# A 2-layer macaron model on one core: the routing and tiles 41 to 52 of the second expert pass take other places in the five engine queues

## The reference, cut to what matters

```python
x = L0_attn_hidden_states                               # 16 x 256 x 128, float32
x = x + 0.5 * _L0_ffn_ref(_layernorm(x), ...)           # 8 experts, top 1: the first passage
x = x + _L0_attn_ref(_layernorm(x), ...)                # conv, q/k/v, cumulative pooling, feed-forward
x = x + 0.5 * _L0_ffn_ref(_layernorm(x), ...)           # the same 8 experts: the second passage
x = x + 0.5 * _L1_ffn_ref(_layernorm(x), ...)           # 16 experts with a capacity
x = x + _L1_attn_ref(_layernorm(x), ...)                # a recurrence along the sequence
x = x + 0.5 * _L1_ffn_ref(_layernorm(x), ...)

def _L0_ffn_ref(x, wr, br, w1, b1, w2, b2):
    expert_id = jnp.argmax(jnp.einsum('bsh,he->bse', x, wr) + br, axis=-1)
    h = gelu(jnp.einsum('bsh,ehf->ebsf', x, w1) + b1)   # 128 -> 512
    y = jnp.einsum('ebsf,efh->ebsh', h, w2) + b2        # 512 -> 128
    return jnp.einsum('ebsh,bse->bsh', y, one_hot(expert_id, 8))
```

## Time and profile before

| | before |
|---|---|
| median of 3 runs | 665.62 us (664.96 to 666.88) |
| the profiled execution | 665.63 us, of which the span is 663.6 |
| PE busy | 612.0 us, 92% of the span |
| DVE busy | 448.8 us, 68% |
| POOL busy | 367.2 us, 55% |
| ACT busy | 323.4 us, 49% |
| mean granted clock of TensorE | 0.957 |

### The profile page before, as it was taken

The page is one execution under the profiler, slowest core; times in us unless marked ns, Lnnn a source line. Parts: engine busy times, 40 slices in busy tenths (PEclk is TensorE's granted clock), DMA queues, the critical chain, the costliest instruction groups (busy, mean ns, idle before and its releaser), DMA issues.

```text
span 663.6 us, 13121 instructions
## 1 busy us (share of the span) xinstructions
PE 612.0 (92%) x3647; PEld 472.9 (71%) x3647; DVE 448.8 (68%) x1882; ACT 323.4 (49%) x1037; POOL 367.2 (55%) x377
## 2 busy tenths in 40 slices
...
GB/s 268 316 153 263 190 210 203 106 50 253 127 60 71 115 42 70 238 201 190 205 254 136 97 147 110 79 144 136 179 11 143 146 57 60 169 115 156 94 100 14
DMA packets 87030, 94.17 MB, mean 142 GB/s; under 512 B 12156, under 2 KB 65439, under 8 KB 86704
## 3 DMA queue, kind: packets, MB, share of 16 engines
...
## 4 chain that ended last, share of the span: by engine, by line
PE 57%; DVE 12%; POOL 12%; DMA 8%; issue 8%; ACT 3%; SPq 1%; ACTq 0%; DVEq 0%; POOLq 0%
PE ps L907 8%; PE ps L900 8%; PE ps L835 8%; PE ps L827 8%; POOL xs L1620 8%; PE ps L932 4%; PE ps L784 3%; PE ps L882 3%; PE ps L745 3%; PE ps L849 3%; POOL y L1624 2%; PE ps L875 2%; DMA y<-yt,xi 2%; PE ps L890 1%; PE ps L914 1%
## 5 line engine op out<-in xcount | busy, mean ns | idle before, releaser
L1620 POOL DMA_INDIRECT xs<-X,IDX x128 | 125.6, 981 | 97.9 <-issue 64.8
L1513 ACT ACTIVATE ht<-ps,CL 128x128 f32<-128x128 f32 x336 | 93.1, 379 | 97.1 <-PE ps L827 97.0
L1624 POOL DMA_INDIRECT y<-yt,xi x84 | 83.1, 989 | 50.1 <-DVE yt L1253 34.7
L827 PE MATMUL ps<-xt,w1s 128*128 128x128 f32 x672 | 86.7, 278 | 1.9 <-DVE xt L1247 1.2
L835 PE MATMUL ps<-W,ht 128*128 (+1 forms) x672 | 86.2, 279 | 2.1 <-ACT ht L1513 1.9
L835 PEld LDWEIGHTS ps<-W,ht 128*128 128x128 f32 x672 | 81.4, 195 | 4.3 <-issue 4.2
L827 PEld LDWEIGHTS ps<-xt,w1s 128*128 128x128 f32 x672 | 80.2, 192 | 4.3 <-DVE xt L1247 2.2
L1611 POOL TENSOR_TENSOR sma<-sma,MH 128x4 f32<-128x4 f32 (+1 forms) x24 | 30.6, 1279 | 69.9 <-DVE sma L962 63.8
L932 PE MATMUL ps<-MT,KC 128*128 128x512 f32 x114 | 55.8, 646 | 0.4
L1570 ACT ACTIVATE hb<-ps 128x320 f32<-128x320 f32 x64 | 26.7, 428 | 49.1 <-PE ps L900 48.8
L1253 DVE SCALAR_TENSOR_TENSOR yt<-ps,xb 128x128 f32<-128x128 f32 x84 | 23.9, 287 | 35.0 <-PE ps L835 33.9
(11 more groups left out here) (214 smaller groups left out, 1299.0 us busy)
## 6 DMA issues: line engine op xcount, KB each, us to landing
...
```

Source lines behind the costliest of these rows:

```text
L827: r = e.matmul(ps[TILE_BANKS[i % n]][:, c * P:(c + 1) * P], W1[i % NW1][:, c * P:(c + 1) * P], XTT[i % NX][:, :], start=True, stop=True)
L1513: r = e.activation(HT[i % NHT][:, c, :], ps[TILE_BANKS[i % len(TILE_BANKS)]][:, c * P:(c + 1) * P], ACT.Gelu, bias=CL[:, bass.ds(r0 * 4 + ...
L1620: return e.indirect_dma_start(dst, bass.IndirectOffsetOnAxis(ap=IDX[:, n:n + 1], axis=0), X[:, n, 0:w], None, bounds_check=hi, oob_is_err= ...
L1624: return e.indirect_dma_start(dst, bass.IndirectOffsetOnAxis(ap=ix, axis=0), src, None, bounds_check=hi_home, oob_is_err=False, engine_sem ...
```

## The change

Only `TABLE` changes. On each of the five lists the steps are the same as before, in another order: on SP places 100 to 144 of 275, on PE 214 to 322 of 766, on DVE 280 to 430 of 865, on ACT 109 to 159 of 382, on POOL 92 to 138 of 304. In words:

- PE: `pscore.8` to `pscore.10` go ahead by some ten places, in between `ak.5`, `aconv.7` and `aturn3.4`; `rrank.2` stands ahead of `ak.6`, `av.6`, `adown.3`, `aturn4.4`, `aturn4.5`, `aturn3.6` and `aup.16` to `aup.18`, not behind them; `tturn.41` to `tup.46` begin earlier among the last attention steps, `adown.7`, `pturn.12`, `pscore.13` to `pscore.15` come later; `rrank.4` stands behind `tup.47` and `tturn.48`, and `tturn.51` ahead of `tup.48`.
- DVE: `pstat.10`, `peps.0`, `plog.3`, `oh.3`, `ra.2`, `rb.2` and `rsel.2` go ahead of attention steps of chunks 4 to 7; the tile steps of 41 to 52 are spread otherwise.
- ACT: a few neighbours change places (`tgelu.41` ahead of `aaff3.7`, `pcopy.11` behind `agelu.30`).
- POOL: `apow3.6` stands behind seven sends, not ahead of all; `ppow` steps move; `home.45` ahead of `send.52`, `home.46` to `home.51` in one run.
- SP: `tload.52` to `tload.58` and `tw.46` to `tw.58` are interleaved otherwise; `tload.53` ahead of `tw.48`.

The diff, cut where both sides are only wrapped otherwise:

```diff
--- before.py
+++ after.py
@@ "sp" @@
-tw.36 tw.37 tw.38 tw.39 tw.40 yload.3 yload.4 yload.5 yload.6 yload.7 fill.0 fill.1 fill.2 fill.3 fill.4 fill.5 fill.6 fill.7 fill.8 fill.9 fill.10
-tw.41 tload.41 tload.42 tload.43 tload.44 tload.45 tload.46 tload.47 tload.48 tw.42 tw.43 tw.44 tw.45 tload.49 tload.50 tload.51 wload.0 wload.1 tw.46
-tw.47 tload.52 tw.48 tw.49 tload.53 tload.54 tw.50 tw.51 tload.55 tw.52 tw.53 tload.56 tw.54 tw.55 tload.57 tload.58 tw.56 tload.59 tw.57 tw.58
+tw.36 tw.37 tw.38 tw.39 tw.40 yload.3 yload.4 yload.5 yload.6 yload.7 fill.0 fill.1 fill.2 fill.3 fill.4 fill.5 fill.6 fill.7 fill.8 fill.9 tw.41
+fill.10 tw.42 tload.41 tload.42 tload.43 tload.44 tload.45 tload.46 tload.47 tload.48 tw.43 tw.44 tload.49 tload.50 tw.45 tw.46 tw.47 tload.51 wload.0
+tload.52 tload.53 wload.1 tw.48 tw.49 tw.50 tw.51 tload.54 tload.55 tload.56 tload.57 tload.58 tw.52 tw.53 tw.54 tw.55 tload.59 tload.60 tw.56 tw.57
+tw.58 tload.61 tload.62 tw.59 tw.60 tw.61 tw.62 tw.63 tload.63 tload.64 tw.64 tload.65 tw.65 tw.66 tload.66 tload.67 tload.68 tw.67 tw.68 tload.69
...
@@ "pe" @@
-aturn2.5 aup.11 aq.4 ak.4 av.4 aturn4.3 adown.2 aq.5 aturn1.7 ak.5 pturn.7 aconv.7 aturn2.6 aturn3.4 av.5 aup.12 aup.13 aturn3.5 aq.6 aup.14 aup.15
-pscore.8 pscore.9 pscore.10 ak.6 av.6 adown.3 aturn4.4 aturn4.5 aturn3.6 aup.16 aup.17 aup.18 rrank.2 aup.19 aturn2.7 adown.4 aq.7 aup.20 aup.21
-aup.22 aup.23 aturn4.6 ak.7 pturn.8 pturn.9 pscore.11 pscore.12 av.7 aup.24 aup.25 aup.26 aturn3.7 aup.27 rrank.3 adown.5 adown.6 aturn4.7 pturn.10
-pturn.11 aup.28 aup.29 aup.30 tturn.41 aup.31 tturn.42 tup.41 tturn.43 adown.7 pscore.13 pscore.14 tturn.44 pturn.12 tup.42 tturn.45 tdown.41 tup.43
-tturn.46 pscore.15 tup.44 tdown.42 tturn.47 tdown.43 tdown.44 rrank.4 tup.45 tup.46 tup.47 tturn.48 tdown.45 tdown.46 tdown.47 tturn.49 tturn.50
-tup.48 tturn.51 tup.49 tup.50 tdown.48 tdown.49 tturn.52 tdown.50 tup.51 tturn.53 tup.52 tup.53 tturn.54 tdown.51 tdown.52 tdown.53 tturn.55 tup.54
-tturn.56 tup.55 tup.56 tturn.57 tdown.54 tdown.55 tturn.58 tdown.56 tturn.59 tup.57 tup.58 tturn.60 tturn.61 tup.59 tdown.57 tdown.58 tdown.59
+aturn2.5 aup.11 aq.4 ak.4 av.4 aturn4.3 adown.2 aq.5 pturn.7 aturn1.7 ak.5 pscore.8 aconv.7 pscore.9 aturn3.4 pscore.10 av.5 aup.12 aturn2.6 aup.13
+aturn3.5 aq.6 aup.14 aup.15 rrank.2 ak.6 av.6 adown.3 aturn4.4 aturn4.5 aturn3.6 aup.16 aup.17 aup.18 aup.19 aturn2.7 aup.20 adown.4 aup.21 aq.7
+aup.22 aup.23 aturn4.6 pturn.8 pturn.9 ak.7 aup.24 pscore.11 pscore.12 av.7 aup.25 aturn3.7 aup.26 aup.27 rrank.3 adown.5 tturn.41 tturn.42 tup.41
+tturn.43 adown.6 aturn4.7 pturn.10 pturn.11 aup.28 aup.29 aup.30 tup.42 tturn.44 tdown.41 tturn.45 aup.31 tup.43 tturn.46 tup.44 tturn.47 tdown.42
+adown.7 tdown.43 tdown.44 tup.45 tup.46 pturn.12 pscore.13 pscore.14 tup.47 pscore.15 tturn.48 tdown.45 tdown.46 rrank.4 tdown.47 tturn.49 tturn.50
+tturn.51 tup.48 tup.49 tup.50 tdown.48 tdown.49 tturn.52 tdown.50 tup.51 tturn.53 tup.52 tup.53 tdown.51 tdown.52 tturn.54 tdown.53 tturn.55 tup.54
+tturn.56 tup.55 tturn.57 tup.56 tdown.54 tdown.55 tturn.58 tdown.56 tturn.59 tup.57 tup.58 tturn.60 tturn.61 tup.59 tdown.57 tdown.58 tdown.59
@@ "dve" @@
-axb.5 ax2.3 ax1.6 astat3.3 astat2.6 anorm3.3 axb2.3 apoolq.4 anorm2.6 apoolk.4 acb.7 amulv.4 aout.2 apoolq.5 pstat.10 apoolk.5 ax1.7 ax2.4 amulv.5
-astat2.7 ax2.5 peps.0 astat3.4 astat3.5 apoolq.6 plog.3 anorm3.4 axb2.4 anorm3.5 apoolk.6 axb2.5 anorm2.7 amulv.6 aout.3 oh.3 ax2.6 ra.2 astat3.6 rb.2
-rte.2 pnm.3 anorm3.6 rsel.2 aout.4 pstat.11 apoolq.7 pstat.12 rslot.2 peps.1 rnext.1 apoolk.7 plog.4 amulv.7 oh.4 ax2.7 ra.3 axb.6 astat3.7 rb.3 pnm.4
-anorm3.7 axb2.6 rsel.3 aout.5 aout.6 rte.3 tn.41 tn.42 pstat.13 pstat.14 tx.41 axb.7 peps.2 tx.42 tn.43 tn.44 axb2.7 txb.41 rslot.3 tx.43 rnext.2
-tn.45 aout.7 txb.42 txb.43 txb.44 tx.44 tn.46 pstat.15 tx.45 pnm.5 peps.3 tn.47 plog.5 ty.41 rslot.4 oh.5 tx.46 plog.6 pnm.6 oh.6 tn.48 ty.42 ra.4
...
+axb.5 ax2.3 ax1.6 astat3.3 astat2.6 anorm3.3 axb2.3 apoolq.4 anorm2.6 apoolk.4 amulv.4 acb.7 aout.2 pstat.10 peps.0 apoolq.5 apoolk.5 ax2.4 plog.3
+ax1.7 amulv.5 astat2.7 ax2.5 astat3.4 astat3.5 oh.3 apoolq.6 anorm2.7 ra.2 rb.2 anorm3.4 apoolk.6 axb2.4 rte.2 anorm3.5 pnm.3 rsel.2 axb2.5 amulv.6
+aout.3 ax2.6 rslot.2 astat3.6 rnext.1 anorm3.6 aout.4 pstat.11 pstat.12 apoolq.7 peps.1 apoolk.7 plog.4 amulv.7 oh.4 tn.41 ax2.7 tn.42 ra.3 axb.6
+astat3.7 rb.3 tx.41 tx.42 pnm.4 tn.43 tn.44 anorm3.7 txb.41 axb2.6 rsel.3 aout.5 tx.43 tn.45 rte.3 aout.6 pstat.13 txb.42 txb.43 txb.44 pstat.14 tn.46
+tx.44 tn.47 axb.7 peps.2 axb2.7 tx.45 ty.41 tx.46 rslot.3 rnext.2 tn.48 tn.49 aout.7 ty.42 ty.43 tx.47 ty.44 pstat.15 peps.3 plog.5 plog.6 txb.45
+pnm.5 oh.5 rslot.4 oh.6 tx.48 pnm.6 ty.45 ra.4 txb.46 ty.46 tn.50 tn.51 rb.4 tx.49 rsel.4 tn.52 tx.50 txb.47 txb.48 txb.49 tx.51 txb.50 tn.53 tn.54
+ty.47 rte.4 ty.48 txb.51 ty.49 tx.52 txb.52 tx.53 txb.53 ty.50 ty.51 txb.54 tx.54 tn.55 tn.56 tn.57 tx.55 ty.52 ty.53 tx.56 tn.58 tn.59 txb.55 ty.54
...
@@ "act" @@
-aaff2.4 aaff2.5 agelu.10 agelu.11 anormA3.3 ares.7 aaff3.3 anormA1.7 aaff1.7 pcopy.7 anormA2.6 aaff2.6 agelu.12 agelu.13 agelu.14 agelu.15 far.0
-anormA3.4 anormA3.5 aaff3.4 aaff3.5 anormA2.7 agelu.16 agelu.17 agelu.18 agelu.19 aaff2.7 anormA3.6 agelu.20 agelu.21 agelu.22 aaff3.6 agelu.23
-pcopy.8 pcopy.9 agelu.24 agelu.25 agelu.26 agelu.27 anormA3.7 aaff3.7 pcopy.10 pcopy.11 agelu.28 agelu.29 agelu.30 agelu.31 tgelu.41 pcopy.12 tgelu.42
+aaff2.4 aaff2.5 agelu.10 anormA3.3 agelu.11 ares.7 aaff3.3 anormA1.7 pcopy.7 aaff1.7 anormA2.6 aaff2.6 agelu.12 far.0 agelu.13 agelu.14 agelu.15
+anormA3.4 anormA3.5 aaff3.4 aaff3.5 anormA2.7 agelu.16 agelu.17 agelu.18 agelu.19 aaff2.7 agelu.20 anormA3.6 agelu.21 agelu.22 agelu.23 aaff3.6
+pcopy.8 pcopy.9 agelu.24 agelu.25 agelu.26 agelu.27 anormA3.7 tgelu.41 aaff3.7 pcopy.10 agelu.28 agelu.29 agelu.30 pcopy.11 agelu.31 tgelu.42 tgelu.43
...
@@ "pool" @@
-home.39 home.40 apow1.2 apow3.1 apow1.3 apow1.4 apow1.5 apow1.6 apow2.2 apow1.7 apow2.3 apow3.2 apow2.4 apow2.5 apow3.3 apow2.6 apow2.7 apow3.4 ppow.0
-apow3.5 apow3.6 send.32 send.33 send.34 send.35 send.36 send.37 ppow.1 send.38 send.39 send.40 send.41 send.42 send.43 apow3.7 send.44 send.45 ppow.2
-send.46 send.47 send.48 send.49 send.50 send.51 ppow.3 home.41 home.42 home.43 home.44 send.52 send.53 send.54 home.45 home.46 home.47 home.48 home.49
-send.55 send.56 send.57 home.50 home.51 send.58 send.59 send.60 send.61 send.62 send.63 home.52 home.53 home.54 home.55 home.56 home.57 home.58
+home.39 home.40 apow1.2 apow3.1 apow1.3 apow1.4 apow1.5 apow1.6 apow2.2 apow1.7 apow2.3 apow3.2 apow2.4 apow2.5 apow3.3 apow2.6 ppow.0 apow3.4 apow2.7
+apow3.5 send.32 send.33 send.34 send.35 send.36 send.37 send.38 apow3.6 send.39 send.40 send.41 send.42 send.43 ppow.1 apow3.7 send.44 send.45 send.46
+send.47 ppow.2 send.48 send.49 send.50 send.51 home.41 home.42 home.43 ppow.3 home.44 home.45 send.52 send.53 send.54 send.55 home.46 home.47 home.48
+home.49 home.50 home.51 send.56 send.57 send.58 send.59 send.60 send.61 send.62 send.63 home.52 home.53 home.54 home.55 home.56 home.57 home.58
```

49 lines of the change are left out of this document (23 added, 26 removed).

## The result

The changed kernel takes 685.59 us (median of 4 runs, 683.69 to 686.98) against 665.29: a ratio of 1.030, 95% interval 1.026 to 1.034. The profiled execution took 684.28 us, its span is 682.9, 19.3 more than before. The forecast was 682.0 in a range of 668 to 688.

The account below looks back on a forecast made before the run. PE and DVE were taken as full where the change begins, POOL behind it. Stalls made aup.16 10.0 us late, adown.7 11.0, tup.63 16.4; span 663.6 + 16.4 = 680.0, with 2.03 around it 682.0 us, range 668 to 688.

Parts of the forecast that it names:

- The sum: Whole kernel: all stalls make tup.63 16.4 us late, span 680.0 us, time 682.0 us.
- First group: First-group routing on PE and DVE: stalls, the largest 4.7 us at rrank.2 and 2.8 at aturn4.4; aup.16 10.0 us late.
- the first group's 10 us: Lag of 10.0 us at aup.16, carried on as part of the 16.4 us at tup.63.
- POOL: apow3.6 behind seven sends: anorm3.6 waits; PE feels 1.2 us at pturn.8, 1.1 at tturn.42, 0.7 at pturn.11.
- Tiles 41 to 52: Stalls of 2.8 us at rrank.4, 1.9 at tturn.50, 2.0 at tturn.51: lag goes from 11.0 to 16.4.
- POOL as the bound at tup.63: At tup.63 POOL's sends bind by 2.5 us: start at 332.1, where PE alone would be there at 329.6.
- The clock rival: PE falls to 1.2 GHz in the rrank.2 stall: 2.5 us more, again at rrank.4 and tturn.50; 684 to 687; chance 0.09.
- a clock of 1.00 in 223 to 240: Sign expected in the changed profile: PE's granted clock stays at 1.00 from 223 to 240 us.
- Faster: If ra.2 is done when PE reaches rrank.2 (223.3), PE waits for nothing: 661.7 or 660 us; chance 0.12.
- No effect: Whole kernel: stalls that appear are the idle time there was, moved; 665.6 us; chance 0.08.

Follow-up runs that it names:

- heat_four: Changed kernel with four matmuls of zeros on PE ahead of rrank.2; one run, +23.6 us against before.
- count_first: Changed kernel with oh.3 and ra.2 moved ahead on DVE, right behind plog.3; one run, +22.8 us against before.
- tiles_only: Order of before up to aup.26 on PE, the changed order from there (rrank.3 and tiles 41 to 52); 1.025 of before.
- tn_late: tiles_only with tn.41 and tn.42 on DVE behind rb.3, not ahead of ax2.7 and ra.3; 1.022 of before.
- pow_first: Changed kernel with apow3.6 on POOL ahead of the sends, as before; one run, +22.5 us against before.
- copy_first: Changed kernel with tx.49 on DVE ahead of rb.4 and tx.50 ahead of rsel.4; one run, +20.8 us against before.
- first_group: Changed order up to rsel.2 on DVE and aturn4.4 on PE, behind that the order of before on all five queues; 1.012 of before.

## Why the prediction came out right, and where it was not

**The sum.** 16.4 us were forecast for the lag at tup.63; it was 18.1, and at the last send 18.0. That it went through is in part chance: behind tup.63 the changed kernel loses 1.5 us more, and before's profile then loses some 2 to its clock. With the 1.55 from ahead of the change that is 19.6; the span grew by 19.3. The forecast let each duration stay and made all of the 16.4 stalls; PE's idle time grew by 9.3 and its busy time by 8.8. That the sum fits has one reason that is no luck: two of the falls of the clock filled waits that had been forecast. (Two slips of the working: PE's idle time of before in 184 to 318 is 134.00 - 129.35 = 4.7 us by the profile's windows, not 5.6, and 285.48 + 16.4 is 301.9, not 302.1.)

**First group: right in its stalls.** pscore.8 waited 0.7 (forecast 1.0), aq.6 0.2 (0.3), rrank.2 4.2 (4.7), aturn4.5 0.1 and aturn3.6 0.4 (0.3 and 0.75); DVE stood 2.49 at ax2.4 (2.6). The wait of aturn4.4 was 1.0 and not 2.8, because ak.6 and av.6 ran at half rate in the meantime: heat_four puts it back to 2.5. aup.16 was 10.4 late (10.0). rsel.2 ended 0.2 earlier (0.3). What PE waits for there is a symptom, as count_first shows: with ra.2 done in time, PE waits for rsel.2 instead.

**The step that failed: what the first group's 10 us are worth.** The prediction carried them through as a term of the sum, as a cause of 10 of the 16 us. tiles_only shows that without them the end is only 0.5 us better in the traces (3 us between the medians, with overlapping intervals). I had looked at what stands behind a step on each queue, but for tn.41, moved ahead of ax2.7 and ra.3, I didn't ask when its input comes: sends from 31.1 on, twelve of 1.28 us, then the landing and the load: not before 52 us behind aq.5, whatever PE does. That is 8.8 us of DVE (tiles_only), and 4.0 us of PE at tturn.41 (tn_late). The sum came out near because these lie beside the first group's 10 and not behind them, which the prediction didn't know: in this the number was luck.

**POOL.** The wait at anorm3.6 was there (3.65 us), but its price was smaller: pturn.8 waited 0.4 us (forecast 1.2), tturn.42 0.9 (1.1) and pturn.11 nothing (0.7). And pow_first, without it, is slower: the edit I charged with 1 us saves 4 in the order that it stands in.

**Tiles 41 to 52: right in place and nearly in size.** The forecast had the lag grow by 5.4 us here, from 11.0 to 16.4; it grew by 6.1 from rrank.3 to tup.48 and by 7.1 to tup.63. The waits were shorter, 0.9 at rrank.4, 1.1 at tturn.50 and 1.5 at tturn.51 (2.8, 1.9 and 2.0), while tdown.45 and tdown.46 took 1.91 and 1.61 us and tup.48 to tup.50 1.44, 1.91 and 1.55, against 1.06 each: 3.1 us at a lower clock. With tdown.45 and tdown.46 at the full clock, in heat_four, the waits are 2.3, 1.2 and 1.4, and tup.48 comes as late behind rrank.3: there the clock cost nothing. What the slow tup.48 to tup.50 cost isn't told apart, since they are slow in every run with this order.

**POOL as the bound at tup.63.** Forecast to bind by 2.5 us, with PE alone 13.9 late (329.6 against 315.74). tup.63 starts 3.9 us behind tload.63 in the changed kernel, tiles_only, copy_first and pow_first, 4.8 before and 6.1 in first_group. That fits the sends as the bound, but PE, 18.1 late, has no idle time just ahead of tup.63, so they are about level there. Three tiles on, the loads do bind: the changed kernel waits 1.52 us at tturn.66, since tn.66 on DVE waited 2.29 for its load; before has no such wait of PE.

**Rivals.** The clock rival had a chance of 0.09 and 684 to 688, and the measured 685.59 lies there, not in the forecast's own 678 to 684. The sign "a clock of 1.00 in 223 to 240" failed: the granted clock in the changed kernel's 227 to 247 is 0.77 to 0.89. But its working, 2.5 us lost at ak.6 to adown.3 and as much at rrank.4 and tturn.50, isn't what happened: at ak.6, av.6 and ahead of rrank.4 the slow rows filled waits. What is left is a part of the 1.4 us at aup.16 and aup.17, and of tup.48 to tup.50 what can't be told apart. And between the changed kernel's four runs the time goes with the clock: 683.69 at a mean of 0.950, 686.98 at 0.938. The Trainium skill, "TensorE: Matmul & The Clock Gate", section "HAM oscillation — how this bites in real kernels", has the engine throttled where bursts have idle time between them; the fall behind the 4.2 us agrees. The fall in 292 to 297 doesn't: the clock is 0.75 there and PE busy for 5.00 of 5.00 us. "Faster" was to be decided by ra.2 being done when PE comes to rrank.2; count_first brought that about, and aup.16 came only 0.5 earlier. "No effect" fell with first_group.
